# Window attention over 4 x 4 pixels: the pixels of a window stand side by side, and the pooled half takes the full half's form

## The reference

```python
xn = group_norm(x, 32 groups)
xw = xn in windows of 4 x 4 pixels            # 4*24*24 windows
qkv = einsum('nchw,oc->nohw', xw, qkv_w)      # 3*128 channels
pooled = avg_pool5(qkv)                       # 5 x 5 sum / 25, within a window, zero padded
for part in (qkv, pooled):                    # 16 heads of 8 channels each
    q, k, v = relu(part_q), relu(part_k), [part_v, 1]
    kv = einsum('ngld,nglm->ngdm', k, v)      # l: the 16 pixels of a window
    out = einsum('ngld,ngdm->nglm', q, kv)
    out = out[..., :-1] / (out[..., -1:] + 1e-15)
y = batch_norm(einsum('nchw,oc->nohw', [out_full, out_pooled], proj_w))
return x + y
```

## Time and profile before

| | |
|---|---|
| median of 3 runs | 960.84 us (960.15 to 962.31) |
| the profiled execution | 960.44 us, of which span 958.5 us |
| busy: PE, DVE, POOL, ACT | 96%, 73%, 68%, 65% |
| DMA | 38.82 MB, 41 GB/s on average |

### The profile page before, as it was taken

How to read it: one execution, slowest core, us unless ns; L and a number is a source line. 1 busy time by engine, 2 the same in 40 slices (tenths; PEclk the granted TensorE clock), 3 DMA queues, 4 the chain that set the end, 5 groups by cost and what they waited for, 6 DMA issues and landing times. The chain is left out here.

```text
span 958.5 us, 48609 instructions
## 1 busy us (share of the span) xinstructions
PE 916.3 (96%) x21026; PEld 727.8 (76%) x21026; DVE 698.8 (73%) x1252; ACT 619.4 (65%) x1541; POOL 655.4 (68%) x1621
## 2 busy tenths in 40 slices
PE   0899999999999999999999999999999999999997
PEld 0677778787777777777777777777777777777775
DVE  7677777876767777787667787878676767676766
ACT  0657676767676666666666666666667676767674
POOL 1667677777777777767676767676767676767671
PEclk9999999999999999999999999999999999999999
DMA  6022220000021211000012121100000000000000
GB/s 254 2 61 65 59 65 25 17 23 19 21 71 50 74 50 57 17 25 17 25 33 74 50 74 50 41 17 25 17 25 17 25 17 25 17 25 17 25 17 34
DMA packets 20645, 38.82 MB, mean 41 GB/s; under 512 B 2416, under 2 KB 15216, under 8 KB 20592
## 3 DMA queue, kind: packets, MB, share of 16 engines
q1 hardware_dynamic: 20592, 38.33, 12.3%
HBM read 19.45 MB, written 18.87 MB: 40 GB/s over the span
## 5 line engine op out<-in xcount | busy, mean ns | idle before, releaser
L404 ACT ACTIVATE q_full<-ps,cst 128x384 f32<-128x384 f32 x192 | 103.4, 590 | 304.4 <-PE ps L723 304.4
L303 POOL TENSOR_TENSOR xd<-x_all,mean_t 128x384 f32<-128x384 f32 x95 | 78.6, 827 | 230.3 <-PE ps L730 211.4
L601 DVE TENSOR_TENSOR kvc_full<-ps,cst 128x864 f32<-128x864 f32 x192 | 193.1, 1046 | 2.2 <-PE ps L742 2.2
L601 DVE TENSOR_TENSOR kvc_pool<-ps,cst 128x864 f32<-128x864 f32 x192 | 192.9, 1045 | 0.0
L607 DVE SCALAR_TENSOR_TENSOR x_all<-ps,shift,x_all 128x384 f32<-128x384 f32 x96 | 59.3, 617 | 168.6 <-PE ps L838 168.6
L703 PE MATMUL ps<-wkv_sb,xn 128*128 128x256 f32 x576 | 142.8, 384 | 23.0 <-DVE xn L556 23.0
L281 POOL TENSOR_TENSOR x_all<-y_pool,x_all 128x96 f32<-128x96 f32 x380 | 147.8, 419 | 15.1 <-ACT y_pool L440 15.1
L723 PE MATMUL ps<-xn,wq_sb 128*128 128x192 f32 x384 | 154.3, 536 | 0.0
L703 PEld LDWEIGHTS ps<-wkv_sb,xn 128*128 128x128 f32 x576 | 102.9, 192 | 33.2 <-issue 23.0
L309 POOL TENSOR_TENSOR xn<-xd,rstd_t 128x96 f32<-128x96 f32 x380 | 121.8, 368 | 8.1 <-DVE xn L556 0.7
L381 ACT ACTIVATE vm_pool<-ps,cst 128x256 f32<-128x256 f32 x288 | 121.9, 552 | 0.0
(11 more groups left out here) (75 smaller groups left out, 1534.1 us busy)
## 6 DMA issues: line engine op xcount, KB each, us to landing
out<-x_all SPq DMA_DIRECT2D x96, 192.0 KB, 1.9
x_all<-x SPq DMA_DIRECT2D x36, 384.0 KB, 3.4
x_all<-x SPq DMA_DIRECT2D x6, 768.0 KB, 7.9
cst<-consts SPq DMA_DIRECT2D x1, 172.0 KB, 11.1
wkv_sb<-wkv SPq DMA_DIRECT2D x1, 128.0 KB, 11.0
wq_sb<-wq SPq DMA_DIRECT2D x1, 128.0 KB, 10.7
o_sb<-proj SPq DMA_DIRECT2D x1, 128.0 KB, 10.4
bn_sb<-bn SPq DMA_DIRECT2D x1, 2.0 KB, 10.5
```

The source lines that it names most:

```text
L404: return act.activation(to, src, ACT.Relu, scale=col(C_SLOT + slot))
L601: last = dve.tensor_tensor(kvc[:, g], src.to_broadcast(shape), own, ALU.mult)
```

## The change

Pixels and windows are laid out anew, the pooled half takes the full half's form, and the order of one ScalarE step changes.

- `xn` holds window after window, each with its 16 pixels in a row, so a conv_q pass reads six runs of 32 neighbouring columns. The masks follow (`win // PAIR` becomes `win % EF` and so on), and the four instructions that write `xn` row by row become one.
- A full tile's pixels come out of the out products in another order, so the transposes of the full half use a permutation (`C_TURN`) for the identity.
- `q_pool` has the layout of `q_full`: a slot of 16 columns per window, of which 9 are used. `out_products_of` serves both halves, with 24 products each. The pooled half has three tiles for two, so the division of the pooled half covers 48 x 8 numbers per partition for 32 x 8, and there are three pooled transposes for two.
- On ScalarE `to_image` and `pooled_out` stand between the two copies of `masked_v_full`.

```diff
-                xr = xn[:, p].rearrange("p (g r c e) -> p r g e c", r=WS, c=WS, e=WIN)
-                xv = xn[:, p].rearrange("p (g r c e) -> p c g e r", r=WS, c=WS, e=WIN)
+                xr = xn[:, p].rearrange("p (w r c) -> p r w c", r=WS, c=WS)
+                xv = xn[:, p].rearrange("p (w r c) -> p c w r", r=WS, c=WS)
...
-                for r in range(WS):
-                    last = pool.tensor_tensor(xr[:, r], rows[:, r], rstd, ALU.mult)
-                last.then_inc(xn_ready, 1)
+                pool.tensor_tensor(xr, rows, rstd, ALU.mult).then_inc(xn_ready, 1)
...
+            def copy_q(q, bank, j, at, first, pairs, mask):
+                to = q[:, at:at + pairs * QS].rearrange("p (n k j) -> p k n j", k=4, j=PX)[:, 0:4:3, :, 0:j]
+                src = ps[:, bank, first:first + 2 * pairs * j].rearrange("p (x n j) -> p x n j", x=2, j=j)
+                return act.activation(to, src, ACT.Relu, scale=col(mask))
...
                 if not is_first(s) and not is_last(s):
-                    masked_v_full(s + 1)
+                    masked_v_full(s + 1, range(1))
                 if not is_first(s):
                     to_image(s - 1)
                     pooled_out(s - 1)
                 if not is_first(s) and not is_last(s):
+                    masked_v_full(s + 1, range(1, EF))
                     relu_k(s + 1)
...
-                full = xn[:, p].rearrange("p (g x a r) -> p r g a x", x=PX, a=EF, r=PAIR)
+                full = xn[:, p].rearrange("p (g r x) -> p r g x", r=PAIR, x=EF * PX)
...
-                    r, w = c // 2, c % 2 * 2 + z
-                    q = QD + (t * 2 + r) * EP * QD + g * QG_AT + Q_AT[w]
-                    last = pe.matmul(ps[Q4 * c:Q4 * (c + 1), OUTP, at:at + n], q_pool[:, q:q + Q4],
-                                     kvc_pool[:, r, (t * G + g) * EP + c % 2 + z], start=z == 0, stop=z == 1)
+            def out_products_of(q, kvc, bank, pairs):
+                n = QG * KC
+                for t in range(TO):
+                    for g in range(G):
+                        at = (t * G + g) * n
+                        for c in range(4):
+                            half, e = divmod(4 * t + c, pairs)
+                            z = QS + (4 * t + c) * QS + g * Q4
+                            last = pe.matmul(ps[Q4 * c:Q4 * (c + 1), bank, at:at + n], q[:, z:z + Q4],
+                                             kvc[:, half % 2, (half // 2 * G + g) * pairs + e], start=True, stop=True)
...
-                        (TRF, o_full, TF, P, C_IDENT, tr_f), (TRP, o_pool, TP, 4 * WP * PXP, C_PACK, tr_p)):
+                        (TRF, o_full, TO, P, C_TURN, tr_f), (TRP, o_pool, TO, 4 * PAIR * PXP, C_PACK, tr_p)):
```

More of the change, by code:

```diff
@@ L50 @@
 C_SLOT_P = C_SLOT + PAIR
-C_PACK = C_SLOT_P + PAIR
+C_TURN = C_SLOT_P + PAIR
+C_PACK = C_TURN + P
 N_CONST = C_PACK + P
@@ L66, in constants @@
     pairs, two = np.arange(EF)[None], np.arange(PAIR)[None]
-    win = (p % (PAIR * EF))[:, None]
-    c[:, C_VF:C_VF + EF] = win // PAIR == pairs
-    c[:, C_KF:C_KF + PAIR] = win % PAIR == two
+    win = (p % H64 // PX)[:, None]
+    c[:, C_VF:C_VF + EF] = win % EF == pairs
+    c[:, C_KF:C_KF + PAIR] = win // EF == two
     win_p = (p % H64 // PXP)[:, None]
@@ L99, in build @@
     assert HALF * KC <= 512 and TF * G * EF == HALF and TP * G * EP == HALF
-    assert WIN_H * PXP <= H64 and QG_AT + Q4 * 2 + PXP * 2 <= QD + Q4
+    assert WIN_H * PXP <= H64
+    TO = HALF // 4
+    assert TO == TF
     FOURS = SPB // 4
@@ L151, in build @@
         q_full = sb("q_full", [QS // 2 + (HALF + 1) * QS])
-        q_pool = sb("q_pool", [QG_AT + (HALF + 1) * QD])
+        q_pool = sb("q_pool", [QS // 2 + (HALF + 1) * QS])
         kvc_full = sb("kvc_full", [G, HALF, QG, KC])
@@ L379, in masked_v, with masked_v_full @@
                 src = src.rearrange("p t (h m) -> p t h m", m=D)
-                for e in range(pairs):
+                for e in pairs:
                     last = act.activation(heads[:, e, :, :, 0:D], src, ACT.Copy, scale=col(masks + e))
                 return last
-            def masked_v_full(s):
+            def masked_v_full(s, pairs=range(EF)):
                 act.wait_ge(conv_f, s + 1)
                 wait(act, kv_f, s)
-                masked_v(vm_full, kv_tiles(KV_F, TF)[:, :, P:], EF, C_VF).then_inc(vm_f, 1)
+                last = masked_v(vm_full, kv_tiles(KV_F, TF)[:, :, P:], pairs, C_VF)
+                if EF - 1 in pairs:
+                    last.then_inc(vm_f, 1)
             def masked_v_pooled(s):
@@ L398, in relu_q @@
                 wait(act, out_f, s)
[L400 to L407, removed]
+                copy_q(q_full, Q_F, PX, QS, PX, HALF, C_SLOT)
+                copy_q(q_full, Q_F, PX, QS // 2, 0, HALF + 1, C_SLOT + 1).then_inc(qm_f, 1)
             def relu_q_pooled(s):
@@ L411, in relu_q_pooled @@
                 wait(act, out_p, s)
[L413 to L421, removed]
+                copy_q(q_pool, Q_P, PXP, QS, PXP, HALF, C_SLOT_P)
+                copy_q(q_pool, Q_P, PXP, QS // 2, 0, HALF + 1, C_SLOT_P + 1).then_inc(qm_p, 1)
             def to_image(s):
@@ L554, in first_strip @@
                 dve.wait_ge(pads_zero, 2)
[L555 to L558, removed]
+                dve.tensor_scalar(xr, rows, mean_t[:, 0:1], rstd_t[:, 0:1],
+                                  ALU.subtract, ALU.mult).then_inc(xn_ready, 1)
                 dve.wait_ge(xn_ready, 1)
@@ L626, in divide @@
             def divide(s, pooled):
-                ready, done, turned, bank, at, tiles, den, o, step = (
-                    (out_p, num_p, tr_p, OUTP, OUTP_AT, TP, den_pool, o_pool, 2) if pooled else
-                    (out_f, num_f, tr_f, OUTF_LAST if is_last(s) else OUTF, 0, TF, den_full, o_full, 0))
+                ready, done, turned, bank, den, o, step = (
+                    (out_p, num_p, tr_p, OUTP, den_pool, o_pool, 2) if pooled else
+                    (out_f, num_f, tr_f, OUTF_LAST if is_last(s) else OUTF, den_full, o_full, 0))
                 dve.wait_ge(ready, s + 1)
-                src = ps[:, bank, at:at + tiles * 16 * HC].rearrange("p (n c) -> p n c", c=HC)
+                src = ps[:, bank, 0:TO * 16 * HC].rearrange("p (n c) -> p n c", c=HC)
                 link(dve.tensor_scalar(den[:], src[:, :, D], DEN_EPS, None, ALU.add), s, step + 1)
@@ L635, in divide @@
                 dve.tensor_tensor(o[:].rearrange("p t (h m) -> p (t h) m", m=D), src[:, :, 0:D],
-                                  den[:].unsqueeze(2).to_broadcast([P, tiles * 16, D]), ALU.mult).then_inc(done, 1)
+                                  den[:].unsqueeze(2).to_broadcast([P, TO * 16, D]), ALU.mult).then_inc(done, 1)
             def step(s, b, at, phase):
@@ L802, in out_products @@
                     pe.nop(nofuse=True)
[L803 to L806, removed]
+                out_products_of(q_full, kvc_full, OUTF_LAST if is_last(s) else OUTF, EF).then_inc(out_f, 1)
             def out_products_pooled(s):
@@ L812, in out_products_pooled @@
                     pe.nop(nofuse=True)
[L813 to L817, removed]
+                out_products_of(q_pool, kvc_pool, OUTP, EP).then_inc(out_p, 1)
             def transposes(s):
```

50 lines of the change are left out of this document (18 added, 32 removed).

## The result

The changed kernel takes 852.02 us in the median of 4 runs (851.35 to 852.42), the kernel before 960.8. The ratio is 0.8865, 95% interval 0.885 to 0.8881. The profiled execution took 852.14, with a span of 850.4. The prediction was 848 with a range from 838 to 878.

A forecast was written before the change was run, and what follows sets the result against it. TensorE's own instructions set 9.35 of the 9.62 us strip period, ScalarE's order 0.27. The terms gave 8.43, taken as 8.45; 95 intervals save 111.2 us, start and tail about 1.4, so 960.8 becomes 848, range 838 to 878.

The forecast's parts named there:

- q reads side by side: Full-size q on TensorE (L723): neighbouring columns cut a pass from 0.355 to 0.163 us, the stage by 0.71 a strip.
- The rival that the step is free: Full-size q on TensorE: the 16-byte step costs nothing, q keeps 1.42 us, period 9.16, time 915; chance 5%.
- 24 products: Pooled out on TensorE: 24 products for 32, 48 pairs for 64, 1.12 us to 0.80, a gain of 0.32.
- The third transpose: Pooled transposes on TensorE: three tiles for two add one transpose, +0.11 us a strip.
- The stall: TensorE's wait at the projection (L838) for ScalarE's copy to o_sb: goes with the new order, 0.27 us a strip.
- rival 4: More gain than counted: 0.10 between L838's two passes vanishes and pooled out runs at 16 ns; period 8.33, 837 us; 5%.
- The touching waits: Handover to pooled kv on TensorE after the full division just touches, +0.02 us; several other waits nearly bind, period taken as 8.45.
- Rival 1: TensorE's waits for o_full or vm_pool, kvc_full and the convolution add up: period 8.65 to 8.75, time 872; chance 16%.
- Sum: TensorE's period per strip: 9.62 - 0.71 - 0.32 + 0.11 - 0.27 = 8.43 us, taken as 8.45.
- Around the period: Start before the first interval and tail after the last q: together a gain of about 1.4 us.
- GpSimd: One xn instruction for four, 1.27 us to 0.83, gain 0.44 at best, nothing at worst, hidden behind waiting.
- VectorE's and GpSimd's rival ways to a slower kernel: GpSimd's xn instructions become the bound, 1042 us if doubled, chance 2%; VectorE's pooled division, +0.27 us, was expected hidden if deadlines hold.

The follow-up runs named there:

- experiment 1: Kernel before with the new pixel layout alone (side-by-side q reads, one xn instruction, permuted transposes); pooled half and ScalarE order as before: 896.16 us.
- experiment 5: Two kernels: the changed one with q passes reading other columns (steps of 4 or 2 elements; runs of 4 or 2 with gaps): 885.42 and 853.36 us.
- experiment 3: Kernel before with only the ScalarE order changed, output copies between the two copies of v: 924.46 us.
- experiment 8: Changed kernel without the reciprocal of the full half, its outputs multiplied by the denominators instead of divided: 849.71 us.
- experiment 6: Changed kernel with VectorE's group statistics of the next image spread over six strips in place of four: 849.44 us.
- experiment 2: Kernel before with the pooled half in the full half's form alone (slots of 16, three pooled tiles): 939.77 us.
- experiment 4: Changed kernel without the new ScalarE order, both copies of v together again ahead of the output copies: 875.83 us.

## Why the prediction came out right

- *q reads side by side:* right in cause and nearly in size, 0.67 for 0.71. A later pass takes 0.162 us as forecast from L703; entering the stage costs 0.10, not 0.06, which was what it cost before (1.43 less four passes of 0.34). The rival that the step is free fell with experiments 1 and 5.
- *24 products:* the term was mis-sized, 0.25 for 0.32, and the stage of 0.86 lies outside the 0.77 to 0.84 that the prediction gave for it. The 17.5 ns a pair were an average that held the way out of the stage: 64 pairs in 1.113 and 48 in 0.862 make 15.7 ns a pair and about 0.11 fixed. The full half's 48 pairs, with pairs of the same form behind them, take 0.774, so 0.09 goes with what follows, the kv products in another form.
- *The third transpose:* 0.11, right.
- *The stall:* 0.27, right, and 0.10 more between the two passes of the projection. The prediction had this as the first half of rival 4, with 5%, and left it out of the sum; it came with the stall's end, in experiment 3 as in the change. The other half, pooled out at 16 ns a pair, didn't come.
- *The touching waits:* +0.03 in pooled kv for +0.02 forecast, and none elsewhere. Rival 1 didn't come about, though two of the waits that it names, for `o_full` and for `vm_pool`, are close to binding (experiment 8). ScalarE waits 2.00 us for q, as forecast.
- *Sum:* 9.62 - 0.67 - 0.02 - 0.25 + 0.11 - 0.27 - 0.10 + 0.03 = 8.45, measured 8.44, forecast 8.45. That 8.45 came out to 0.01 is luck in part: two errors of 0.04 and 0.07 on one side met 0.10 and 0.02 on the other.
- *Around the period:* the prediction was 4 us too low here. It named the strips with two statistics instructions, which cost nothing, and overlooked those with the group statistics, 2.4 us in all (experiment 6). And it counted the start as a gain, where the clock's fall turned an earlier beginning into 1.4 us of loss.
- *GpSimd:* one xn instruction takes 0.83, for 1.27, hidden, as said. VectorE's and GpSimd's rival ways to a slower kernel didn't come near.

The 946.7 us from which the prediction works out the period isn't in the earlier trace rows, which print the loads of weights (946.3). It stands in the row of the matmuls, and the 9.62 is right:

```profile
L723 PE MATMUL ps<-xn,wq_sb x384: 518/519/587, 31.7 to 946.7; 128*128 128x192 f32 x192
```

The parts alone: 0.69 (experiment 1), 0.22 (2) and 0.38 (3) off the period, 1.29 in all, against 1.18 for the three together. The third transpose, hidden in experiment 2 by the stall that experiment 3 removes, is the difference.

## What to carry to other kernels

Before counting instructions, divide the distance between starts by the columns, stage by stage: the one stage with twice the time a column was the largest gain. Before multiplying an average by a number of instructions removed, split it into what each costs and what the stage costs once, from two stages of different length. And when a steady loop is made shorter, look also for the few iterations that carry more work than the others: they had slack before and may have none after.

## What the runs showed of the hardware

- TensorE's fp32 moving operand: 340 ns for 192 columns when each 16 bytes touched give one column in succession, 170 with two, 162 with four (experiment 5 and the changed kernel).
- A wait ahead of two matmul passes costs 0.10 us between the passes on top of the gap: the two passes of the full projection take 0.75 with the wait (before, experiments 1, 2, 4) and 0.64 without (experiment 3, changed).
- At the start, behind 1.2 us of idle time, the second strip's six passes took 2.0 to 2.8 us in eight traces of eight; with 0.15 us or none there, 1.5 us in five of five. Behind 1.9 us of idle time in the second step the clock fell to 1.2 GHz in five traces of nine.
